# Experts: 49 tiles of 256 rows and eight of 128 in place of 56 of 256

## The reference, cut to what matters

```python
N, D, E, H = 6250, 256, 8, 1024
logits = xt @ Wr + br
top_p, top_idx = top_k(softmax(logits), 2)
weights = top_p / top_p.sum(-1)
xe = layernorm(xt) * ln_g[e] + ln_b[e]                   # for each expert e
h  = gelu(xe @ W1[e] + b1[e])                            # 256 -> 1024
y  = h @ W2[e] + b2[e]                                   # 1024 -> 256
out = x + sum over the node's two experts of weights * y
```

## Time and profile before

| | us |
|---|---|
| median of 3 runs | 1972.28 |
| lowest, highest | 1969.89, 1974.74 |
| profiled execution | 1967.06 |
| its span, first to last instruction | 1965.4 |
| expert stage, from its first layer two on | 1280.8 to the end |

### The profile page before, as it was taken

The page is one execution under the profiler, slowest core; times in us unless marked ns, Lnnn a source line. Parts: engine busy times, 40 slices in busy tenths (PEclk is TensorE's granted clock), DMA queues, the critical chain, the costliest instruction groups (busy, mean ns, idle before and its releaser), DMA issues. The chain is left out here.

```text
span 1965.4 us, 32482 instructions
## 1 busy us (share of the span) xinstructions
PE 1592.8 (81%) x8582; PEld 1315.7 (67%) x8583; DVE 1123.4 (57%) x3118; ACT 909.9 (46%) x1979; POOL 1138.3 (58%) x1141
## 2 busy tenths in 40 slices
PE   6766667667777777887777836799999999999997
PEld 5655455555655545465555635689999999999996
DVE  6622222222345466675665667667777777777774
ACT  6611111111214233344443478656666666666664
POOL 3177777777777677777777627753333333333333
PEclk9978888888888899998988955589999999999999
DMA  8344444344347666666777558498888788878885
GB/s 218 116 128 126 109 121 117 114 120 122 112 141 230 207 201 212 201 211 208 224 213 222 142 183 275 166 314 224 219 217 217 218 223 221 216 214 216 218 222 127
DMA packets 188121, 368.81 MB, mean 188 GB/s; under 512 B 33325, under 2 KB 134173, under 8 KB 173657
## 3 DMA queue, kind: packets, MB, share of 16 engines
q0 software_dynamic: 77296, 252.50, 46.2%
q1 hardware_dynamic: 102992, 113.64, 18.2%
q10 hardware_dynamic: 7736, 1.52, 0.4%
HBM read 287.94 MB, written 80.39 MB: 187 GB/s over the span
## 5 line engine op out<-in xcount | busy, mean ns | idle before, releaser
L699 POOL DMA_INDIRECT w2s_lent<-z_d,edge_tabs_lent x784 | 776.3, 990 | 289.2 <-issue 239.0
L1317 DVE TENSOR_TENSOR acc_lent<-acc_lent,bank 128x258 f32 x244 | 102.5, 420 | 477.9 <-PE bank L1816 474.3
L1816 PE MATMUL bank<-w2s_lent,G 128*128 x976 | 282.4, 441 | 111.4 <-POOLq L687 111.4
L1816 PE MATMUL bank<-w2s_lent,S_lent 128*128 x976 | 270.6, 426 | 85.6 <-POOLq L687 84.1
L2026 PE MATMUL bank<-w2s 128*128 128x512 f32 x896 | 330.6, 403 | 2.8 <-DMA w2s<-w_d 2.8
L1816 PEld LDWEIGHTS bank<-w2s_lent,G 128*128 128x128 f32 x976 | 208.8, 220 | 176.9 <-issue 139.6
L1816 PEld LDWEIGHTS bank<-w2s_lent,S_lent 128*128 128x128 f32 x976 | 202.3, 213 | 150.0 <-issue 115.1
L743 POOL DMA_INDIRECT out_dram<-G,acc_lent x112 | 179.7, 1605 | 209.3 <-DVE G L1650 170.5
L1040 ACT ACTIVATE G<-bank,acc_lent 128x256 f32<-128x256 f32 x448 | 188.0, 471 | 195.2 <-PE bank L2007 109.1
L2005 PE MATMUL bank<-w2s,acc 128*128 128x256 f32 x896 | 258.9, 289 | 3.7 <-DVE w2s L1629 3.0
L2006 PE MATMUL bank<-w2s,acc 128*128 128x256 f32 x896 | 253.7, 283 | 0.0
(11 more groups left out here) (318 smaller groups left out, 2572.0 us busy)
## 6 DMA issues: line engine op xcount, KB each, us to landing
w2s<-w_d POOLq DMA_DIRECT2D x112, 1024.0 KB, 5.6
w_d<-w2s_lent SPq DMA_DIRECT2D x64, 256.0 KB, 3.7
acc_lent<-bucket_d SPq DMA_DIRECT2D x56, 266.0 KB, 2.8
w2s_lent<-z_d,edge_tabs_lent POOLq DMA_INDIRECT x784, 2.9
bu_d<-w2s_lent SPq DMA_DIRECT2D x98, 128.0 KB, 1.9
w2s_lent<-bu_d SPq DMA_DIRECT2D x14, 768.0 KB, 8.2
w1s<-in_L_ffn_W_dram SPq DMA_DIRECT2D x8, 1024.0 KB, 6.6
w2s_lent<-in_L_ffn_W_dram SPq DMA_DIRECT2D x32, 256.0 KB, 5.2
```

Source lines behind the costliest of these rows:

```text
L699: pool.indirect_dma_start(out=ring_rows[:, row % (RING * QUAD), 0:D], out_offset=None, in_=z_d[:, :], in_offset=bass.IndirectOffsetOnAxis( ...
L1317: dve.tensor_tensor(to, to, bank[j % DEPTH][:, 0:ACCW], ALU.add).then_inc(s["acc_done"], 1)
L1816: m = pe.matmul(bank[j % DEPTH][:, 0:ACCW], S_of[j % DEPTH][:, k, :], rows[:, ds(bases[j], ACCW)], start=(k == 0), stop=(k == QUAD - 1))
```

## The change

Buckets are counted in units of 128 rows. 49 tiles keep 256 rows; eight tiles have 128, the tiles 8, 15, 22 and so on to 50, and the last, 56. A bucket with an odd number of units has its last unit in a small tile; small tiles that are left over serve as halves. The table has the large tiles in its first slots and the small ones from slot 64 on, for which DVE computes `slots` once and a longer `last_tiles`. A small tile's load, transposes, gelu, remainders, second products, weighing and adds are of 128 rows; its layer one has the same 48 products, of 128 columns. Its weights are split and loaded as for a large tile. All bodies are written out, with constants in place of loop registers. One semaphore, `srcf_ready`, is merged into another.

```diff
-MOE_TILES = (2 * N + EXPERTS * (MT - 1)) // MT
+UNITS = (2 * N + EXPERTS * (P - 1)) // P
+BIG = (UNITS - EXPERTS + 1) // 2
+MOE_TILES = BIG + EXPERTS
+SMALL_AT = [8 + 7 * k for k in range(EXPERTS - 1)] + [MOE_TILES - 1]
+SMALL_SLOT = 64
...
-        def moe_tiles(eng, links, body):
-
-            def two(turn):
-                body(2 * turn, 0)
-                body(2 * turn + 1, 1)
-            for turn in range(1, EARLY // 2 - 1):
-                two(turn)
-            eng.wait_ge(s["moetab_set"], 2)
-            repeat(eng, links, two, EARLY // 2 - 1, MOE_TILES // 2 - 1)
-            body(MOE_TILES - 2, 0)
-            body(MOE_TILES - 1, 1)
+        def moe_tiles(eng, body):
+
+            for i in range(2, MOE_TILES):
+                if i == EARLY - 2:
+                    eng.wait_ge(s["moetab_set"], 2)
+                body(i, i % 2)
+
+        def small(t):
+            return t in SMALL_AT
+
+        def halves(t):
+            return 1 if small(t) else 2
+
+        def slot_of(t):
+
+            if small(t):
+                return SMALL_SLOT + SMALL_AT.index(t)
+            return t - sum(at < t for at in SMALL_AT)
+
+        def added(t):
+
+            return 16 * sum(halves(k) for k in range(t))
...
+            return eng.value_load(moetab[0:1, P + slot_of(t):P + slot_of(t) + 1], min_val=0, max_val=EXPERTS - 1)
+
+        def hidden(v, t, q):
+
+            v = v[:, q * 2 * MT:(q + 1) * 2 * MT].rearrange("p (k n) -> p k n", n=MT)
+            return v[:, :, 0:P] if small(t) else v
...
-            def load_xe(t, h, turn):
-                r = sp.value_load(moetab[0:1, ds(t, 1)], min_val=0, max_val=PADROW)
+            def load_xe(t):
+                h, n = t % 2, halves(t)
+                r = sp.value_load(moetab[0:1, slot_of(t):slot_of(t) + 1], min_val=0, max_val=PADROW)
                 until(sp, s["xe_free"], t - 1)
-                sp.dma_start(xe[h], bucket_d[ds(r, MT), :].rearrange("(j p) w -> p j w", p=P)).then_inc(pair["xe_in"][h], 16)
-
-            def load_xes(turn):
-                for h in range(2):
-                    load_xe(2 * turn + h, h, turn)
+                sp.dma_start(xe[h][:, 0:n, :], bucket_d[ds(r, n * P), :].rearrange("(j p) w -> p j w", p=P)).then_inc(pair["xe_in"][h], 16)
...
-            repeat(sp, None, load_xes, EARLY // 2, MOE_TILES // 2)
-            sp.wait_ge(s["y_add"], 16 * 2 * MOE_TILES)
+            for t in range(EARLY, MOE_TILES):
+                load_xe(t)
...
-                until(pool, s["y_add"], 32 * t)
+                until(pool, s["y_add"], added(t))
...
                 for g in range(2):
-                    if in_range(i, -1):
+                    if in_range(i, -1) and g < halves(i - 1):
                         add_y(i - 1, 1 - par, g)
...
-            for g in range(2):
-                add_y(MOE_TILES - 1, 1, g)
+            moe_tiles(pool, moe)
+            for g in range(halves(MOE_TILES - 1)):
+                add_y(MOE_TILES - 1, (MOE_TILES - 1) % 2, g)
...
+                        w = halves(i + 1) * P
                         for k in range(2):
-                            g = act.activation(raw[q % 2][:, k * MT:(k + 1) * MT], bank[q % 2][:, k * MT:(k + 1) * MT], ACT.Gelu,
+                            g = act.activation(raw[q % 2][:, k * w:(k + 1) * w], bank[q % 2][:, k * w:(k + 1) * w], ACT.Gelu,
...
+                        act.activation(hidden(hhi, i + 1, q).bitcast(F32R), hidden_raw(i + 1, q), ACT.Copy).then_inc(s["h_hi"], 1)
...
+            def slots():
+
+                L.after(dve.tensor_scalar(small_no, pcol, float(SMALL_SLOT), None, ALU.is_ge))
+                L.after(dve.tensor_scalar(at_slot, pcol, -0.5, BIG - SMALL_SLOT / 2, ALU.mult, ALU.add))
+                dve.tensor_scalar(less_half, small_no, -0.5, None, ALU.mult)
+                L.after(dve.scalar_tensor_tensor(out=at_slot, in0=small_no, scalar=at_slot, in1=pcol, op0=ALU.mult, op1=ALU.add))
+                L.after(dve.tensor_scalar(small_no, small_no, -1000.0, 1000.0 - SMALL_SLOT, ALU.mult, ALU.add))
+                L.after(dve.tensor_tensor(small_no, small_no, pcol, ALU.add))
...
-                whole_tiles(cf, MT - 1)
-                L.after(dve.tensor_tensor(dl8, ntf, early_of[:, 1:EXPERTS + 1], ALU.subtract))
-                L.after(dve.tensor_scalar(dl8, dl8, -float(MT), float(CAP), ALU.mult, ALU.add))
-                L.after(dve.tensor_tensor(ntf, ntf, early_of[:, 0:EXPERTS], ALU.subtract))
+                L.after(dve.tensor_scalar(ci, cf, float(P - 1), None, ALU.add))
+                L.after(dve.tensor_scalar(ci, ci, 7, None, ALU.logical_shift_right))
+                dve.tensor_copy(units, ci)
...
+                dve.scalar_tensor_tensor(out=tile_table[:, 0:1], in0=rc_odd, scalar=is_odd, in1=rc, op0=ALU.mult, op1=ALU.add)
+                dve.scalar_tensor_tensor(out=tile_table[:, 1:2], in0=ec_odd, scalar=is_odd, in1=ec, op0=ALU.mult, op1=ALU.add
+                                         ).then_inc(s["mtab_ready"], 1)
...
-                L.after(dve.tensor_copy(xhi[par].bitcast(F32R), bank[4][:, :]))
+                rows = bank[4][:, 0:halves(t) * DC * P].rearrange("p (k n) -> p k n", k=DC)
+                hi, lo = (v[par][:, 0:halves(t) * DC * P].rearrange("p (k n) -> p k n", k=DC) for v in (xhi, xlo))
+                L.after(dve.tensor_copy(hi.bitcast(F32R), rows))
                 dve.tensor_copy(b1c[par], b1T[:, ds(e * HC, HC)])
-                dve.tensor_tensor(xlo[par].bitcast(F32R), bank[4][:, :], xhi[par], ALU.subtract).then_inc(s["xs_ready"], 1)
+                dve.tensor_tensor(lo.bitcast(F32R), rows, hi, ALU.subtract).then_inc(s["xs_ready"], 1)
...
-                until(dve, s["y_add"], 32 * (t - 1))
-                dve.tensor_copy(nid[par].rearrange("p (j o) -> p j o", o=1), wid[par][:, :, 1:2])
-                for j in range(2):
+                until(dve, s["y_add"], added(t - 1))
+                n = halves(t)
+                dve.tensor_copy(nid[par][:, 0:n].rearrange("p (j o) -> p j o", o=1), wid[par][:, 0:n, 1:2])
+                for j in range(n):
...
+                        dve.tensor_tensor(hidden(hlo, i + 1, q).bitcast(F32R), hidden_raw(i + 1, q), hidden(hhi, i + 1, q),
+                                          ALU.subtract).then_inc(s["h_split"], 1)
...
+                w = halves(t) * P
                 for c in range(DC):
-                    for j in range(2):
-                        m = pe.transpose(bank[4][:, c * MT + j * P:c * MT + (j + 1) * P], xe[par][:, j, c * P:(c + 1) * P], ident[:, :])
+                    for j in range(halves(t)):
+                        m = pe.transpose(bank[4][:, c * w + j * P:c * w + (j + 1) * P], xe[par][:, j, c * P:(c + 1) * P], ident[:, :])
...
+                    c, w = 2 * q + half, halves(t) * P
+                    to = bank[q % 2][:, half * w:(half + 1) * w]
                     for k in range(DC):
                         hi, lo = (v[:, k, c * P:(c + 1) * P].bitcast(F32R) for v in (w1hi, w1lo))
-                        x_hi, x_lo = (v[par][:, k * MT:(k + 1) * MT].bitcast(F32R) for v in (xhi, xlo))
+                        x_hi, x_lo = (v[par][:, k * w:(k + 1) * w].bitcast(F32R) for v in (xhi, xlo))
...
-                    for to in y_banks[par]:
+                    for to in y_banks[par][0:halves(t)]:
...
-                    for j, to in enumerate(y_banks[par]):
+                    for j, to in enumerate(y_banks[par][0:halves(t)]):
...
-            for turn in range(1, EARLY // 2 - 1):
-                two(turn)
-            pe.wait_ge(s["moetab_set"], 2)
-            repeat(pe, None, two, EARLY // 2 - 1, MOE_TILES // 2 - 1)
-            moe(MOE_TILES - 2, 0)
-            moe(MOE_TILES - 1, 1)
+            moe_tiles(pe, moe)
```

More of the change, by code:

```diff
@@ L329, in build_program @@
         early_rows = tiny2(2)
+        less_half, at_slot, small_no = (tiny2(1) for _ in range(3))
         small3 = [xTs[:, :], edge_tabs[:, RT * PAYW:2 * P * EJ]]
@@ L722, in load_w2l @@
                 e = expert_of(pool, t)
-                if not isinstance(t, int) or t > 1:
+                if t > 1:
                     pool.wait_ge(s["l2_done"], MOE_PARTS * (t - 2) + 2 * g + 2)
@@ L1596, in last_tiles @@
             def last_tiles():
-                rc, ec = ss6[:, 0:1], ss6[:, 1:2]
+                rc, ec, rc_odd, ec_odd, is_odd, at = (ss6[:, k:k + 1] for k in range(6))
                 dve.wait_ge(s["mtab_cnt"], 2)
@@ new lines, in last_tiles @@
+                L.after(dve.tensor_scalar(ci, ci, 7, None, ALU.logical_shift_right))
+                dve.tensor_copy(units, ci)
+                L.after(dve.tensor_scalar(row8.bitcast(I32), ci, 1, None, ALU.logical_shift_right))
+                L.after(dve.tensor_copy(ntf, row8.bitcast(I32)))
+                dve.scalar_tensor_tensor(out=row8, in0=ntf, scalar=float(MT), in1=eoff, op0=ALU.mult, op1=ALU.add)
+                L.after(dve.scalar_tensor_tensor(out=odd, in0=ntf, scalar=-2.0, in1=units, op0=ALU.mult, op1=ALU.add))
@@ new lines, in last_tiles @@
```

(5 more changed lines are left out.)

91 lines of the change are left out of this document (43 added, 48 removed).

## The result

| | before | after |
|---|---|---|
| median, us | 1970.31 (8 runs) | 1954.88 (8 runs) |
| lowest to highest | 1966.06 to 1974.74 | 1949.79 to 1960.81 |
| profiled execution, us | 1967.06 | 1954.48 |
| ratio, 95% interval | | 0.9928 [0.9914, 0.9943] |

The change makes the kernel faster, by 15.4 us between the medians and by 14 us (11 to 17) by the ratio. The forecast was 15.4 us less, and with it 1956.9 us, counted from the median of 1972.28 us that three runs of before had given; eight runs give 1970.31.

A forecast was written before the change was run, and what follows sets the result against it. PE's time per tile was taken to bound the expert stage. Terms -13.3 (tiles), -2.1 (end), 0 (table) and 0 (other engines) gave -15.4 us, from 1972.28 to 1956.9 us, range 1953 to 1965.

The forecast's parts named there:

- Narrow products: Layer one of small tiles: each 128-column product paced by its weight load, 0.112 us, with ends 0.109 and 0.120.
- rival on PE: Layer one of small tiles: products at 0.22 us, 1998 us, chance 0.07; or at 0.060 us, 1937 us, chance 0.06.
- three rows: Plain f32 products in the trace before: 0.110 us at 8 columns, 0.119 at 130, 0.109 at 128 with single-column loads.
- A small tile: PE's time per small tile in the expert stage: 5.38 + 2.82 + 0.32 = 8.52 us, against 12.04 for a large one.
- The path: PE's tiles in the expert stage: 16.12 us less, of which 13.3 count, the last tile's layer two being off the path.
- The loop: Loop over the expert tiles: costs PE nothing, so writing all tiles out gains nothing by itself.
- Rows 4: Trace rows read as the last two tiles, written out and not in the loop, lying 12.04 us apart.
- The table: `last_tiles` on DVE grows from 15 instructions to 28: up to 2.7 us, taken as 0 because covered.
- the idle stretch that I named: Soon after `last_tiles`, DVE idles 2.61 us for ACT's weights; said to cover the longer table.
- VectorE in the short bodies: Bodies with small layer two: DVE might hold PE, 0 taken, up to 8.5 us, 1965 us; rival's chance 0.12.
- just met: Short bodies: the 2.76 us margin of the next tile's transposed rows, less 2.9 us, with DVE entering 0.6 us earlier.
- The end: Behind the last tile: one add less, 1.84 us, and a half-width last residual; together 2.1 us less.

The follow-up runs named there:

- e2: Kernel after, with layer one of a small tile streaming only 64 of its 128 columns; stretch 634.45 us against 634.59, one run 1965.88 us.
- e3: Kernel after, with layer one of a small tile loading only 64 of each 128 weight columns; stretch 18.08 us shorter, one run 1937.26 us.
- e4: Kernel after, with layer one of small tiles streaming 256 columns again; stretch 3.75 us longer, median 1958.85 us.
- e1: Kernel before, with its three loops over the tiles written out; ratio to before 1.0005, median 1969.14 us.
- e7: Kernel after, with VectorE's copy of the next tile's turned rows made five times in seven short bodies; stretch 20.24 us longer, one run 1982.33 us.
- e9: Kernel after, with a small tile's narrow layer-one products placed between the other tile's wide layer-two ones; stretch 2.98 us longer, median 1960.15 us.
- e11: Kernel after, with the low part of small tiles' layer-one weights in 16 bits; stretch 4.92 us shorter, median 1951.22 us, ratio to before 0.9904.

## Why the prediction was right, and where it was off

- **Narrow products.** 0.112 us taken, 0.111 measured, and e2 and e3 show the reason that the prediction gave. Neither rival on PE has anything left, not 0.22 us and not 0.060. The Trainium skill gives 81 ns (TensorE: Matmul & The Clock Gate, section Back-to-back issue gap); for f32 weights the trace speaks against that figure, and the measurement decides. Of the prediction's three rows, though, only the one of 8 columns can tell a load from columns. The products of 128 columns at 0.109 us have a load of a single column, 84 ns long and not 189, so there the columns of plain f32 set the pace: 0.85 ns each, by which 130 take 0.111 us as well. For rounded f32 it is 0.46 (layer two's 0.235 us for 512 columns; e3 has 0.06 us for 128). That the two rows came out beside the load's 0.110 us is chance.
- **A small tile.** 8.52 us taken, 8.44 measured (12.04 - 3.60). The narrowing of layer one saves 0.48 us by e4 where 0.38 were taken; the rest is as taken. The path: -13.3 taken, -13.69 measured.
- **The loop.** Said to cost nothing; e1 shows it. Rows 4, read as the last two tiles, are the two ahead of the last one, which starts at 1947.46; the 12.04 us between them stand.
- **The table.** 0 taken, up to 2.7 bounded. VectorE's part ends 1.7 us later than the 1283.99 of before, and layer two of tile 1 starts at 1298.80 where it started at 1299.18. No cost shows, there or in the starts of tile 1 of the other profiles. What covers it is wider than the idle stretch that I named: PE waits there for the second weights.
- **VectorE in the short bodies.** The reading "just met" was right: 2.7 to 3.0 us of margin in the bodies of before and 3.0 or more in the long ones of after, 0.8 in short ones, and PE has no wait there. The price of missing it was put too low: I allowed for each short body the time by which it is missed, and e7, which misses it by 2.2 us, lost 2.9 for each, since the clock fell as well.
- **The end.** This is the term that was off. The add less was worth 2.29 us (2.1 taken), but I let the sum stop at the landing of the last add, as if what follows were a constant. It isn't: in the kernel after, with 106 adds, it is 3.76 us longer, in GpSimd's DRAIN. The term is +1.5 us and not -2.1.

So the sum of the profiled pair is -12.6 us against -15.4: the last term is 3.6 us off, and the others give some of it back. That the medians differ by just 15.4 us is the luck of runs that spread over 9 and 11 us. The 2 us by which 1956.9 missed 1954.88 are those by which the median of before moved from three runs to eight.

## What to carry to other kernels

A product with few moving columns costs what the next load of stationary weights costs, so halving a tile pays mostly on the side where its rows are the weights; cheaper loads (fewer columns, a 16-bit type) help, another order doesn't. Work taken off the bounding engine shortens the other engines' margins in the same body: read them as the time from the last step that feeds it to the first instruction that reads it. Measure such a change over the steady stretch, since what comes before can vary by 12 us, nearly the gain, and don't take the time behind the last transfer for a constant.

## What the runs showed of the hardware that was not expected

- A load is only one product ahead: with wide products between the narrow ones nothing more is hidden (0.69 us for a group of five in either order, e9).
- A column of plain f32 costs 0.85 ns (0.109 us for 128), one of rounded f32 0.46 (0.235 us for 512).
- Behind three of seven stops of PE of 2 us the granted clock fell to 1.2 GHz, at some 1.5 us each (e7).
- A load of 128 16-bit columns takes 96 ns against 189 for f32, 12 ns more than one of a single f32 column: not the columns alone count but their type too (e11, and the 0.027 us above).
- The DMA engines' busy share doesn't scale with what they move: 219 GB/s at 0.81, 291 GB/s at 0.96.
- The time from the last indirect add to the end of the program is 5.4 us with 112 adds, 9.0 to 9.2 with 106, and 4.4 in another kernel with 112.
